# A two-layer graph network on one core: moving the addition of the edges' x from POOL's DMAs to VectorE

## The chip, the cores and the metric

The kernel runs on one core of one Trainium2 chip. The metric is the device time of one execution, in microseconds. Inputs and outputs lie in the chip's memory; intermediate tables are kept there too.

## What is computed

There are 100,000 nodes with rows of 64 fp32 numbers, and 25,000 edges (src, dst), sorted by dst. Two layers follow each other.

```
h = relu(layernorm(x))
# layer 0: attention over the incoming edges of a node, residual branch, batch norm over the nodes
score = sum(h[src] * h[dst]);  a = softmax of score over the edges of one dst
agg   = segment_sum((h @ W_conv + b_conv)[src] * a, dst)
r     = relu(h @ W_res + b_res)
x2    = x + batchnorm(agg + r) * gamma + beta
h2 = relu(layernorm(x2))
# layer 1: messages along the edges, summed at dst, combined with the node
m     = gelu(gelu([h2[src], h2[dst], edge_attr] @ W_m1 + b_m1) @ W_m2 + b_m2)
boxes = segment_sum(m, dst)
out   = x2 + h2 + gelu(gelu([h2, boxes] @ W_c1 + b_c1) @ W_c2 + b_c2)
```

## The kernel before

Nodes are worked in 49 steps of 2048 (the last has 1696: 106 partitions of 16 rows). Edges are worked in G = 49 groups: a group is 128 partitions by 4 edges; the last has 106 partitions. Each engine has its own program, in an order written out by hand, two steps or two groups a round; semaphores tie them together. There are three stages.

Stage A (0 to about 865 us) goes over all nodes and all edges of layer 0. SyncE (SP) loads x; VectorE (DVE) centres it and scales it; TensorE (PE) transposes and multiplies by W_res; ScalarE (ACT) applies relu, and stores r. For each group, GpSimd (POOL) issues eight indirect DMAs (`gather_x`, L605): for each of 4 edge columns the rows x[dst] and x[src], 128 rows of 256 bytes each, into a ring of GS = 8 tiles (`x_ring`, two of its own, two in `gout`, four in `part`). SP stores each ring tile to the table `edge_x` (`stash_x`, L433), and the edges' r goes to the table `edge_r`. DVE must have centred a ring tile before POOL may gather into it again (`E_ctr`, waited for in `gather_x`). The groups are taken from the last to the first. The attention sums of a group, divided (L838 to L842), stay in SBUF (`agg`). From the 31st group on, POOL also scatters them to the table `agg_rows` (`put_agg`, four indirect DMAs a group, L609), one group after each third group of gathers, and then 18 groups (`PUTS_AHEAD`) without any step between. An index above N - 1 marks a row that is left out, so the scatters, and in the kernel before also the gathers, carry a bounds check against a register.

Stage B (about 865 to 1375 us) goes over the nodes: x2, its layer norm, the two products of the combining network, and the output rows of all nodes as if they had no incoming edge. POOL adds h2 to x2 of the even steps (`add_h2`, L648) and between two such steps issues the rest of the scatters to `agg_rows`, and once all have landed, from 1107 us on, gathers agg[src] for the edges (`gather_agg`, four indirect DMAs a group) into a ring of 4; SP stores these to `edge_agg` (`stash_agg`, L538). POOL may gather into a ring slot when its store has landed.

Stage C (about 1375 us to the end) goes over the groups again. SP loads `edge_r` to `rr` (L510) and `edge_agg` to `agg_in` (L516). DVE's `scale_r` (L997, L999) adds agg[src] to the src half of `rr` and multiplies all of it by the batch norm's scale. Then POOL's `add_x` (L642) issues a direct DMA that adds the stored x rows to `rr` in SBUF; PE's `sum_edges` (L1553, L1556) waits for its landing (`C_x`), and sums `rr` and the filled agg of dst to x2 of the edges. DVE centres it (L772, L774), and the messages follow: PE products, ACT gelus, a scan on DVE along the sorted edges (L1033), and the combining network. POOL writes the finished rows of the dst nodes over `out` (`put_final`, L609, four scatters a group; `edge_final`, L1041, on DVE makes them ready). In POOL's loop over g the order is add_x(g), then gather_agg for a group 34 ahead, then up to two put_final per g from g = 15 on. The messages are summed with indices of `prev_row`, a table of flags loaded by SP (`load_prev`).

## Time and profile before

| | us |
|---|---|
| three runs | 1833.20, 1814.08, 1828.24 |
| their median | 1828.24 |
| the profiled execution | 1824.53 |
| its span, first to last instruction | 1822.7 |

The profiled execution's own time is 1.8 us above its span. In a profile PE is TensorE's matmuls, PEld its weight loads, DVE VectorE, ACT ScalarE, POOL GpSimd, SP SyncE; an engine's name with q is its sequencer, which issues DMAs. A row of a timeline gives start, duration, engine, line, operation, tiles, and in brackets how long the engine had been idle and what released it. "issue" means that the profile shows nothing that was waited for; "remote" or "another core or an unknown queue" that a semaphore was waited for whose update the profile can't put down to an instruction. POOL's busy time covers the making of a DMA's descriptors, not its transfer; there are 0.3 us between two indirect DMAs on POOL that count as idle.

### The profile page before, as it was taken

Reading aid. Unit: us, or ns where it says so; the run is one execution under the profiler, and the core shown is the slowest. Engines: PE = TensorE matmul, PEld = TensorE weight load, DVE = VectorE, ACT = ScalarE, POOL = GpSimd, SP = SyncE. Lnnn points to the kernel's source line nnn. Section 1 sums busy time; section 2 is a strip of 40 time slices with the busy share of each in tenths; the row PEclk is TensorE's granted clock in tenths of the full one; section 3 lists DMA queues with packets and bytes.
Section 4 is the critical chain, followed back from the end, with each engine's and each line's share of the span. In section 5 each row is a group of like instructions: output and inputs, shape, how many; then the busy total and the mean of one; then the engine's idle time right before and its main releaser. Section 6 shows DMA issues by size and latency. Waiting matters only on the chain.

```text
span 1822.7 us, 22166 instructions
## 1 busy us (share of the span) xinstructions
PE 1313.4 (72%) x6521; PEld 875.2 (48%) x6521; DVE 1351.0 (74%) x2253; ACT 927.7 (51%) x1840; POOL 1233.3 (68%) x1062
## 2 busy tenths in 40 slices
PE   3441756765737475275898898888885998899994
PEld 1231545554526354164666666566664443444431
DVE  7832776798649387187979998688854998799972
ACT  4511533453325242163666776476651776577772
POOL 7774664677765747500868887667867878887675
PEclk8755776786778676587888997798875999899996
DMA  7751764654435332125344554555555764566620
GB/s 216 258 177 34 285 231 155 209 200 141 117 95 166 100 114 90 36 99 220 110 160 157 194 185 161 163 176 189 174 160 127 183 162 121 133 146 156 139 49 16
DMA packets 132615, 273.56 MB, mean 150 GB/s; under 512 B 30404, under 2 KB 47658, under 8 KB 132496
## 3 DMA queue, kind: packets, MB, share of 16 engines
q1 hardware_dynamic: 76004, 187.38, 30.8%
q0 software_dynamic: 39360, 43.42, 12.0%
q10 hardware_dynamic: 17132, 41.35, 6.1%
q8 instruction: 54, 0.88, 0.2%
q14 instruction: 65, 0.53, 0.1%
HBM read 151.68 MB, written 121.80 MB: 150 GB/s over the span
## 4 chain that ended last, share of the span: by engine, by line
PE 29%; issue 24%; POOL 18%; another core or an unknown queue 10%; DVE 10%; ACT 5%; DMA 3%; ACTq 0%; SPq 0%; POOLq 0%; DVEq 0%
POOL agg_rows L609 11%; PE banks L1503 4%; POOL out L609 4%; PE banks L1387 3%; PE banks L1579 2%; DVE stat L772 2%; PE banks L1372 2%; PE banks L1577 2%; PE banks L1493 2%; PE banks L1586 2%; DVE stat L764 2%; PE banks L1553 2%; PE banks L1593 2%; POOL agg_ring L605 2%
## 5 line engine op out<-in xcount | busy, mean ns | idle before, releaser
L605 POOL DMA_INDIRECT part<-in_x,edge_idx x192 | 212.1, 1104 | 124.1 <-DVE part L774 66.3
L605 POOL DMA_INDIRECT agg_ring<-agg_rows,edge_idx x196 | 233.5, 1191 | 84.8 <-issue 56.4
L609 POOL DMA_INDIRECT agg_rows<-agg,put_first x196 | 232.2, 1185 | 58.0 <-issue 57.6
L609 POOL DMA_INDIRECT out<-agg,put_last x196 | 215.5, 1100 | 67.3 <-issue 59.8
L1503 PEld LDWEIGHTS banks<-packed,cT 97*128 97x128 f32 (+1 forms) x1568 | 216.3, 223 | 45.1 <-issue 45.1
L1372 PE MATMUL banks<-ident,xc 128*128 128x128 f32 (+1 forms) x784 | 137.6, 326 | 136.6 <-issue 76.4
L1503 PE MATMUL banks<-packed,cT 97*128 97x64 f32 (+1 forms) x1568 | 224.4, 309 | 0.0
L1099 ACT ACTIVATE hT<-banks 128x512 f32<-128x512 f32 (+1 forms) x98 | 55.5, 594 | 324.0 <-remote 165.4
L1387 PE MATMUL banks<-hT,packed 128*128 128x512 f32 (+1 forms) x196 | 132.2, 810 | 78.9 <-issue 54.3
L1372 PEld LDWEIGHTS banks<-ident,xc 128*128 128x128 f32 (+1 forms) x784 | 113.9, 177 | 147.5 <-issue 100.6
L1493 PE MATMUL banks<-hT,packed 64*96 64x512 f32 (+1 forms) x392 | 127.7, 730 | 59.6 <-ACT cT L1216 45.9
L605 POOL DMA_INDIRECT x_ring<-in_x,edge_idx x104 | 118.2, 1137 | 56.5 <-issue 34.1
L605 POOL DMA_INDIRECT gout<-in_x,edge_idx x96 | 106.0, 1104 | 45.1 <-issue 28.6
L764 DVE TENSOR_REDUCE stat<-sq 128x16 f32<-128x1024 f32 (+1 forms) x98 | 117.4, 1213 | 24.0 <-ACT sq L1091 19.4
L648 POOL TENSOR_TENSOR xt<-xt,xc 128x1024 f32<-128x1024 f32 (+1 forms) x19 | 49.2, 2589 | 120.9 <-DVE xc L778 120.6
L838 DVE RECIPROCAL inv<-banks 128x4 f32<-128x4 f32 (+1 forms) x49 | 8.7, 177 | 152.8 <-remote 134.4
L778 DVE SCALAR_TENSOR_TENSOR xc<-xc,stat 128x1024 f32<-128x1024 f32 (+1 forms) x98 | 117.1, 1217 | 1.7
L1091 ACT ACTIVATE sq<-xc 128x1024 f32<-128x1024 f32 (+1 forms) x98 | 102.8, 1049 | 29.9 <-issue 19.6
L772 DVE TENSOR_REDUCE stat<-xt 128x16 f32<-128x1024 f32 (+1 forms) x86 | 104.1, 1210 | 11.0 <-POOL xt L648 7.9
L774 DVE SCALAR_TENSOR_TENSOR xc<-stat,xt 128x1024 f32<-128x1024 f32 (+1 forms) x86 | 109.1, 1268 | 2.9
L1432 PE MATMUL banks<-agg,ones 128*128 128x256 f32 (+1 forms) x98 | 41.3, 512 | 91.1 <-DVE agg L842 88.0
L1215 ACT ACTIVATE cT<-banks,packed 96x512 f32<-96x512 f32 (+1 forms) x98 | 66.7, 681 | 76.6 <-PE banks L1493 72.7
(166 smaller groups left out, 3195.2 us busy)
## 6 DMA issues: line engine op xcount, KB each, us to landing
xt<-in_x SPq DMA_DIRECT2D x84, 512.0 KB
r_rows<-rT ACTq DMA_DIRECT2D x48, 512.0 KB
agg_rows<-rb SPq DMA_DIRECT2D x48, 512.0 KB
out<-xt SPq DMA_DIRECT2D x36, 512.0 KB
edge_r<-rr ACTq DMA_DIRECT2D x48, 256.0 KB
rT<-r_rows SPq DMA_DIRECT2D x24, 512.0 KB
part<-r_rows SPq DMA_DIRECT2D x24, 512.0 KB
rr<-edge_r SPq DMA_DIRECT2D x48, 256.0 KB
```

Source lines behind the costliest of these rows:

```text
L605: A.indirect_dma_start(to, None, table[:, :], bass.IndirectOffsetOnAxis(ap=idx, axis=0), bounds_check=limit, oob_is_err=False).then_inc(si ...
L609: A.indirect_dma_start(table[:, :], bass.IndirectOffsetOnAxis(ap=idx, axis=0), rows_of, None, bounds_check=limit, oob_is_err=False).then_i ...
L764: V.tensor_reduce(total, rows(squares), AX, ALU.add).then_inc(st.sem, 1)
L772: V.tensor_reduce(total, rows(source), AX, ALU.add).then_inc(st.sem, 1)
L774: V.scalar_tensor_tensor(out=rows(tile), in0=per_row(total), scalar=-1.0 / D, in1=rows(source), op0=ALU.mult, op1=ALU.add).then_inc(st.sem, 1)
L778: V.scalar_tensor_tensor(out=tile, in0=source, scalar=0.0, in1=per_row(deviation), op0=ALU.max, op1=ALU.mult).then_inc(st.sem, 1)
L1091: A.activation(sq[s % 2][0:p, :], xc[s % CS][0:p, :], ACT.Square).then_inc(st.sem, 1)
L1215: A.activation(blocks(cT[b][0:H2, 0, :], p), blocks(bank(4)[0:H2, :], p), ACT.Gelu, bias=bc1[:, :])
L1372: ins = T.transpose(to[:, c:c + p], xc[s % CS][0:p, c:c + P], ident[0:p, 0:p])
L1387: T.matmul(blocks(W[0][:, c], p), wres2[:, :], blocks(hT[:, c], p), start=True, stop=True)\
L1493: ins = T.matmul(blocks(bank(4 + i)[0:H2, :], p), wc1_node[i * D:i * D + D, :], blocks(hT[i * D:i * D + D, b * HALF:(b + 1) * HALF], p), s ...
L1503: ins = T.matmul(to[0:p, i * D:i * D + D], cT[b][:, i % 2, (i // 2) * P:(i // 2) * P + p], wc2[:, :], start=(i == 0), stop=(i == 7))
```

## The change

Three things are changed. In stage C, SP loads the stored x rows of a group to the first four tiles of the ring (`x_in`; the last two of them are in use by stage B until its last step), and DVE adds them to the scaled `rr` in a third instruction of `scale_r`; PE waits for DVE's count instead of the DMA, and POOL's 49 adding DMAs are gone. The gathers lose their bounds check, the scatters keep it. All indirect DMAs of the last group take 128 partitions instead of 106; the index table holds 0 for edges that don't exist, which the scatters leave out, and DVE sets the group's `agg` to zero at the start.

```diff
--- before.py
+++ after.py
@@ -203,6 +203,7 @@
         outT = [rT[1][:, q * EG:(q + 1) * EG] for q in range(2)]
         pairT = [sq[q // 2][:, (q % 2) * EG:(q % 2 + 1) * EG] for q in range(4)]
         x_ring = [sb(f"x_ring{q}", [P, EC]) for q in range(2)] + [gout[0][:, 0:EC], gout[0][:, EC:2 * EC]] + xe
+        x_in = x_ring[0:4]
         agg_in = [sb(f"agg_in{q}", [P, EW]) for q in range(MI)]
         agg_ring = [sb(f"agg_ring{q}", [P, EW]) for q in range(RS)]
 
@@ -294,12 +295,12 @@
 
         C_ld = Slots(E_st.sems, before=G)
         C_ga = slots("gathered_agg_loaded", MI)
-        C_x = slots("edge_x_added", 4)
+        C_x = slots("edge_x_loaded", 4)
         C_ea = slots("edge_attr_loaded", 4)
         C_sm = slots("same_prev_loaded", MS)
         C_ft = stage("agg_transposed")
         C_fs = stage("agg_filled")
-        C_ra = stage("edge_r_scaled", 2)
+        C_ra = stage("edge_r_scaled", 3)
         C_as = stage("edge_x2_summed")
         C_xd = stage("dst_x2_copied")
         C_f = stage("edge_x2_centered", 2)
@@ -515,6 +516,13 @@
                 sp.wait_ge(Y_st.of(g), Y_st.after(g))
                 sp.dma_start(agg_in[g % MI][0:p, :], edge_agg[g][0:p, :]).then_inc(C_ga.of(g), 16)
 
+            def load_edge_x(g):
+                C_ra.done(sp, g - 4)
+                if g in (2, 3):
+                    sp.wait_ge(B_fin.sem, B_fin.after(S - 1))
+                p = edges_of(g)
+                sp.dma_start(x_in[g % 4][0:p, :], edge_x[g][0:p, :]).then_inc(C_x.of(g), 16)
+
             def load_attr(g):
                 c = edges_of(g) * EJ
                 q = (g % 4) * DE
@@ -555,6 +563,8 @@
                     for g in range(2):
                         load_prev(g)
                     for g in range(6):
+                        if g < 2:
+                            load_edge_x(g)
                         if g < 4:
                             load_attr(g)
                             load_agg(g)
@@ -573,9 +583,11 @@
                 a = 2 * i
                 if i == 0:
                     for g in range(2, 4):
+                        load_edge_x(g)
+                    for g in range(2, 4):
                         load_prev(g)
-                for g, do in ((a + 4, load_agg), (a + 6, load_edges), (a + 5, load_agg), (a + 7, load_edges),
-                              (a + 4, load_prev), (a + 5, load_prev)):
+                for g, do in ((a + 4, load_agg), (a + 4, load_edge_x), (a + 6, load_edges), (a + 5, load_agg),
+                              (a + 5, load_edge_x), (a + 7, load_edges), (a + 4, load_prev), (a + 5, load_prev)):
                     if is_group(g):
                         do(g)
                 due = max(stashed, min(G, agg_groups(S - 1) - G + a + 3))
@@ -602,8 +614,7 @@
                 pool.reg_add(limit, nodes, -1)
 
             def gather(to, table, idx, signal):
-                A.indirect_dma_start(to, None, table[:, :], bass.IndirectOffsetOnAxis(ap=idx, axis=0),
-                                     bounds_check=limit, oob_is_err=False).then_inc(signal, 16)
+                A.indirect_dma_start(to, None, table[:, :], bass.IndirectOffsetOnAxis(ap=idx, axis=0)).then_inc(signal, 16)
 
             def scatter(table, idx, rows_of, signal):
                 A.indirect_dma_start(table[:, :], bass.IndirectOffsetOnAxis(ap=idx, axis=0), rows_of, None,
@@ -611,35 +622,27 @@
 
             def gather_x(n):
                 g = group_of(n)
-                p = edges_of(g)
                 E_ctr.done(pool, n - GS)
                 X_st.done(pool, n - GS)
                 waits_end()
                 for j in range(EJ):
                     for k, idx in enumerate((dst_idx, src_idx)):
                         c = (2 * j + k) * D
-                        gather(x_ring[n % GS][0:p, c:c + D], x, idx_of(idx, g, j, p), G_x.of(n))
+                        gather(x_ring[n % GS][:, c:c + D], x, idx_of(idx, g, j, P), G_x.of(n))
 
             def put_agg(n):
                 g = group_of(n)
-                p = edges_of(g)
                 G_p.done(pool, n - 4)
                 pool.wait_ge(E_f.sem, E_f.after(n))
                 waits_end()
                 for j in range(EJ):
-                    scatter(agg_rows, idx_of(put_first, g, j, p), agg_of(g, p)[:, j * D:(j + 1) * D], G_p.of(n))
+                    scatter(agg_rows, idx_of(put_first, g, j, P), agg_of(g, P)[:, j * D:(j + 1) * D], G_p.of(n))
 
             def gather_agg(g):
-                p = edges_of(g)
                 Y_st.done(pool, g - RS)
                 waits_end()
                 for j in range(EJ):
-                    gather(agg_ring[g % RS][0:p, j * D:(j + 1) * D], agg_rows, idx_of(src_idx, g, j, p), G_a.of(g))
-
-            def add_x(g):
-                p = edges_of(g)
-                C_ra.done(pool, g)
-                A.dma_start(rr[g % 6][0:p, :], edge_x[g][0:p, :], accum_op=ALU.add).then_inc(C_x.of(g), 16)
+                    gather(agg_ring[g % RS][:, j * D:(j + 1) * D], agg_rows, idx_of(src_idx, g, j, P), G_a.of(g))
 
             def add_h2(s):
                 p = nodes_of(s)
@@ -648,12 +651,11 @@
                 A.tensor_tensor(here, here, xc[s % CS][0:p, :], ALU.add).then_inc(B_y.sem, 1)
 
             def put_final(g):
-                p = edges_of(g)
                 C_put.done(pool, g - 4)
                 pool.wait_ge(C_fin.sem, C_fin.after(g))
                 waits_end()
                 for j in range(EJ):
-                    scatter(out, idx_of(put_last, g, j, p), agg_of(g, p)[:, j * D:(j + 1) * D], C_put.of(g))
+                    scatter(out, idx_of(put_last, g, j, P), agg_of(g, P)[:, j * D:(j + 1) * D], C_put.of(g))
 
             for n in range(G):
                 if n == 0:
@@ -680,7 +682,6 @@
             last = G - ahead
             put = 0
             for g in range(G):
-                add_x(g)
                 if is_group(g + ahead):
                     gather_agg(g + ahead)
                 if g == last:
@@ -718,6 +719,7 @@
                     st.part(dve, step, k[0])
                 return done
 
+            V.memset(agg_of(G - 1, P), 0.0)
             V.memset(bias16[:, :, :], 0.0)
             for b in range(2):
                 V.memset(cT[b][H2:H2 + 1, :, :], 1.0)
@@ -997,6 +999,9 @@
                 V.tensor_tensor(to, to, rows(agg_in[g % MI][0:p, :]), ALU.add).then_inc(C_ra.sem, 1)
                 dve.wait_ge(C_ra.sem, C_ra.after(g, 1))
                 V.tensor_tensor(here, here, cols(bn[0:p, 0, :], ER), ALU.mult).then_inc(C_ra.sem, 1)
+                dve.wait_ge(C_x.of(g), C_x.after(g))
+                dve.wait_ge(C_ra.sem, C_ra.after(g, 2))
+                V.tensor_tensor(rr[g % 6][0:p, :], rr[g % 6][0:p, :], x_in[g % 4][0:p, :], ALU.add).then_inc(C_ra.sem, 1)
 
             def fill_scan(g):
                 c_ = edges_of(g) * EJ
@@ -1549,7 +1554,7 @@
                 if g == 0:
                     pe.wait_ge(B_ht.sem, B_ht.after(S - 1))
                     pe.wait_ge(s_fill, 6)
-                pe.wait_ge(C_x.of(g), C_x.after(g))
+                pe.wait_ge(C_ra.sem, C_ra.after(g))
                 T.matmul(to, ident[0:p, 0:p], rr[g % 6][0:p, :], start=True, stop=False)
                 pe.wait_ge(C_fs.sem, C_fs.after(g))
                 for j in range(EJ):
```

## Rows read from the trace of the kernel before

**Rows 1.** The page's head: busy time of each engine, POOL by fortieths of the span.
```profile
PE 1313.4 (72%) x6521; PEld 875.2 (48%) x6521; DVE 1351.0 (74%) x2253; ACT 927.7 (51%) x1840; POOL 1233.3 (68%) x1062
...
POOL 7774664677765747500868887667867878887675
```
**Rows 2.** Windows: stages A and C, two stretches of A; PE, PEld, DVE, ACT, POOL busy, clock.
```profile
0.00:865.00 865.00, 478.46 (x2329) 370.07 (x2329) 580.65 (x1054) 327.72 (x644) 516.24 (x472) 0.71 0.46 155
...
1375.00:1823.00 448.00, 387.07 (x1468) 172.27 (x1468) 349.44 (x667) 276.71 (x711) 332.48 (x306) 0.91 0.53 125
...
680.00:764.00 84.00, 30.52 (x138) 23.93 (x136) 37.35 (x72) 13.54 (x27) 65.12 (x63) 0.58 0.23 75
764.00:860.00 96.00, 64.39 (x370) 53.38 (x370) 72.49 (x149) 45.56 (x89) 0.40 (x1) 0.80 0.39 146
```
**Rows 3.** Timeline of stage A: one DVE stall and POOL beside it, one ACT stall.
```profile
121.06 1.81 PE L1404 MATMUL banks<-packed,sums 65*128 65x65 f32 x8
169.23 0.18 DVE L838 RECIPROCAL inv<-banks 128x4 f32<-128x4 f32 x1 [49.12 <-remote]
164.26 1.00 POOL L605 DMA_INDIRECT part<-in_x,edge_idx  x1 [0.30 <-issue]
187.98 1.00 POOL L605 DMA_INDIRECT part<-in_x,edge_idx  x1 [22.72 <-DVE part L774]
751.79 0.60 ACT L1099 ACTIVATE hT<-banks 128x512 f32<-128x512 f32 x1 [43.09 <-remote]
763.43 0.97 POOL L609 DMA_INDIRECT agg_rows<-agg,put_first  x1 [0.30 <-issue]
```
**Rows 4.** Waits of DVE in stage A: total us, times, longest.
```profile
DVE inv L838 <- remote: 134.4, 9, 49.1
```
**Rows 5.** POOL's DMAs by tile: ns min/median/max, first and last start us.
```profile
L605 POOL DMA_INDIRECT part<-in_x,edge_idx x192: 991/997/2936, 57.5 to 682.7; - x192
L609 POOL DMA_INDIRECT agg_rows<-agg,put_first x196: 966/972/2826, 451.4 to 1100.0; - x196
L642 POOL DMA_DIRECT2D rr<-edge_x x49: 883/1003/1037, 1376.6 to 1747.0; - x49
```
**Rows 6.** POOL's timeline: of the last group (106 partitions): first and eighth gather, first and last scatter.
```profile
4.85 1.79 POOL L605 DMA_INDIRECT x_ring<-in_x,edge_idx  x1 [3.30 <-issue]
...
20.63 1.62 POOL L605 DMA_INDIRECT x_ring<-in_x,edge_idx  x1 [0.30 <-issue]
...
451.39 2.83 POOL L609 DMA_INDIRECT agg_rows<-agg,put_first  x1 [0.30 <-issue]
1815.62 1.56 POOL L609 DMA_INDIRECT out<-agg,put_last  x1 [0.31 <-issue]
```
**Rows 7.** PE's timeline at the opening of stage C: its waits for the adding DMA.
```profile
1386.96 2.04 PE L1553 MATMUL banks<-rr,ident 128*128 128x512 f32 x2 [12.76 <-DMA rr<-edge_x]
1402.10 1.19 PE L1553 MATMUL banks<-rr,ident 128*128 128x512 f32 x1 [7.37 <-DMA rr<-edge_x]
```
**Rows 8.** Windows of stage C: the stretch with stalls, and the steady one.
```profile
1500.00:1575.00 75.00, 63.57 (x234) 29.06 (x233) 56.19 (x107) 44.29 (x113) 60.12 (x57) 0.91 0.49 119
1600.00:1745.00 145.00, 144.57 (x583) 64.57 (x582) 136.01 (x255) 107.11 (x281) 109.87 (x102) 1.00 0.62 142
```
**Rows 9.** DVE's timeline in stage C: scale_r of three groups, idle gaps, the tail.
```profile
1494.71 0.69 DVE L999 TENSOR_TENSOR rr<-rr,bn 128x512 f32<-128x512 f32 x1
1615.99 0.69 DVE L999 TENSOR_TENSOR rr<-rr,bn 128x512 f32<-128x512 f32 x1
1642.55 0.69 DVE L764 TENSOR_REDUCE stat<-esq 128x8 f32<-128x512 f32 x1 [0.23 <-issue]
1737.22 0.69 DVE L999 TENSOR_TENSOR rr<-rr,bn 128x512 f32<-128x512 f32 x1
1779.45 0.69 DVE L764 TENSOR_REDUCE stat<-esq 106x8 f32<-106x512 f32 x1 [6.61 <-issue]
```
**Rows 10.** DVE adds in stage B, by tile: ns min/median/max, first and last start.
```profile
L961 DVE TENSOR_TENSOR xt<-xt,gout x37: 1210/1217/3940, 878.7 to 1374.0; 128x1024 f32<-128x1024 f32 x36, 106x1024 f32<-106x1024 f32 x1
```

## The prediction

> **What bounds the kernel now.** I read the page first. No engine is busy over 74% of the span, and the digits of POOL hang at 6 to 8 through all of it [rows 1]. That looks like slack and isn't: two indirect DMAs on POOL start 1.30 us apart, of which 1.00 counts as busy and 0.30 as idle [rows 3], so POOL issuing without a pause shows 77%.
>
> The windows by stage come next [rows 2]. Stage A is the worst: 865 us for 581 us of DVE and 478 of PE, the clock at 0.71 on average. The timeline shows why. PE's last matmul of L1404 ended by the profile at 122.9 us, yet DVE, which waits for it at L838, starts at 169.23, with 49 us put down to nobody. POOL had issued gathers without a gap until 164.26 + 1.00, and then waited for a ring slot [rows 3]. Late in the stage ACT stood for 43 us with POOL in a row of 72 scatters; these ended at 764.4, and then, with POOL idle (0.4 us busy of 96), DVE was busy 72 of 96 us, against 37 of 84 just before [rows 2, 3]. DVE's waits of this kind at L838 alone are 134 us in 9 times [rows 4]. So I read stage A as set by POOL's streams of indirect DMAs: while one runs, PE's semaphore updates arrive late, and each stall ends when POOL pauses. Why that is so the trace doesn't say.
>
> In stage C the steady stretch is different: PE busy 144.6 of 145 us, DVE 136.0 [rows 8]. L999 at 1615.99 and 1737.22 are 16 groups, 8 rounds, apart: 15.15 us a round [rows 9]. PE bounds it with DVE right behind. Before that, from 1500 to 1575, PE is busy only 63.6 of 75 us [rows 8].
>
> **Part 1: POOL's 49 adding DMAs go, SP loads, DVE adds.** Saved first:
> - The opening of stage C. PE waits 12.8 and then 7.4 us for the adding DMA [rows 7]. The x of groups 2 and 3 can't be loaded before stage B's last rows are ready, behind SP's stores of gathered agg, and DVE's in-order queue stands at its third add until they land: all four scale_r are ahead of the first fill_scan. So I leave the first wait as it is and take away the second, less 2 us of that queueing: -5 us.
> - The middle. Once the final scatters start, POOL issues 8 of them and one add per group, 8 x 1.27 + 1.3 = 11.5 us, for groups that come every 7.6 us. The eight groups after L999 at 1494.71 take to 1570.4, 75.7 us against 4 x 15.15 = 60.6: -15 us. With no add in its loop POOL can be late only for the output rows, which nobody on the chip waits for until the end.
> - The tail. POOL catches up its puts in one row after its last add at 1747 us [rows 5], and DVE stands for 6.6 us at L764 [rows 9]. With the adds gone the puts are not behind. I take half: -3 us.
>
> Added: 49 adds of 128x512 on DVE, both inputs in SBUF. The nearest row is L999, the same tile, 0.69 us [rows 9]; it depends on the one before, which costs a gap of 0.03 us: 0.72 each. Four stand ahead of the rounds where DVE waits for loads anyway; 45 in them. Two a round are 1.44 us. DVE's idle time in a round is (145 - 136.0) / 145 x 15.15 = 0.94 us, of which nine dependent steps of the inversion take some 0.3 at 0.03 each; 0.23 is a wait for ACT's square [rows 9] that an add standing ahead of it covers. I take 0.3 us of cover in all, so DVE becomes the bound at 15.15 + 1.14 = 16.3 us a round: 22.5 x 1.14 = +26 us. Ends: all idle time but the gaps covers (22.5 x 0.8 = +18), or none (45 x 0.72 = +32).
>
> SP's new loads stand behind nothing long: x of group a+4 waits for DVE's third instruction of group a, done two rounds earlier, and is issued before SP stops at load_edges. Behind it wait load_edges and load_prev of later groups, a round or more ahead of use. Bytes moved by DMA stay the same. I price this at 0; one late load of a few us a round is the upper end, and nothing below 0.
>
> The SBUF page of the Trainium skill (SBUF — State Buffer, on which operations grab the shared port pair) says that a DVE instruction with two SBUF inputs contends with a GpSimd one that reads SBUF, and the later blocks fully. L961, which has two, takes 1.22 us as a rule and up to 3.94 us in stage B, where POOL has adds of its own [rows 10]; that agrees. By that rule each new add could meet a POOL add and take 2.7 us more, but stage C has none, only DMAs, so the sum stays.
>
> Sum of part 1: -5 - 15 - 3 + 26 = +3 us.
>
> **Part 2: gathers without the bounds check.** 392 gathers in stage A, 196 later. The trace has no unchecked indirect DMA. The scatter, also checked, takes a median of 0.972 us against 0.997; the direct DMA, 128 rows of descriptors with no check and no index, has a median of 1.003 and a minimum of 0.883 [rows 5]. So the check is at most 0.11 us by the latter, 0.41 if the 0.30 us between indirect DMAs is its price too (the direct DMA starts without that gap), and less than nothing if the unchecked form is slower, by 0.03 at most as far as the forms differ here. I take 0.03 us, since the two kinds differ by no more. In stage A, which POOL sets: 384 x 0.03 = -11.5 us. In B the 136 gathers after 1107 us share the path with PE: half of 4, -2. In C they are hidden.
>
> **Part 3: a full last group.** With 106 partitions the eight first gathers took 1.79 to 1.62 us (15.3 in all), the first scatter 2.83 (7.7 with the three after it), the last of the kernel 1.56, as did the three before it to 0.03 [rows 6]. With 128 they should take 0.97 to 1.00. The gathers come to 8.0, so 7.3 less, of which I count half, since nodes alone fill the first three rounds: -3.5. First scatters: 7.7 - 3.9 = -4, in a POOL stream of stage A. Last four: 4 x 0.6 = -2.4, fully on the end. The memset at the start of DVE lies before the first x has landed: 0. Sum -10.
>
> **Sum.** 1824.5 + 3 - 13.5 - 10 = 1804, against the profiled execution's own time; that execution is 0.2% under the median of the three runs, 1828.2. I predict 1805 us. About 1% is what a measurement of this kernel can tell from no change (the runs before span 19 us).
>
> **Rivals.**
> 1. The check was dear. If the 0.30 us gap goes with it, stage A loses 384 x 0.30 = 115 us more than 0, B about 10: 1824.5 + 3 - 10 - 125 = 1690. At 0.1 us it is 38 + 5 + 10 - 3: 1770. For it: the gap stands ahead of indirect DMAs only. Against: scatter, gather and direct DMA take nearly the same time, and the gap may be the reading of the indices.
> 2. Slower: stage C gets stage A's disease. Today its indirect DMAs come in rows of 4 or 8 with a direct one between, and PE loses nothing in the steady stretch. Without it POOL issues rows as long as it has ready groups; about three groups are behind when the puts begin. In stage A, DVE lost 134 us at L838 over 764 us of POOL streams, 18%. Over the 274 us of final scatters (196 x 1.4) that would be +48, over half of them +24. With DVE's adds uncovered (+32), and nothing from the check: 1824.5 + 32 - 5 - 15 - 2.4 + 24 = 1858. It decides from the point where POOL is more than a group behind all through the stage. Against: production of a group takes 8 us and its puts 5.6, so POOL must pause in each round once it has caught up.
> 3. Break-even: stage A doesn't follow POOL after all (its stalls have another cause), the unchecked gather costs the same, and only part 1 and the tail count: 1824.5 + 3 - 2.4 = 1825.
>
> **Chances.** My forecast's own case 0.36 (1788 to 1818), rival 1 0.24, rival 2 0.22, rival 3 0.18. Faster by over 1% (below 1810) takes rival 1 and six tenths of my case: 0.46. Slower by over 1%: 0.22. Within: 0.32. The range runs from 1735, between rival 1's two figures, to 1856.
>
> **What would show it.** Stage C: L999's spacing 16.3 us a round instead of 15.15, DVE at 98% and PE near 92% in the steady stretch, no PE wait at L1553 over 5 us after the first. POOL: no L642; the last four scatters at 0.97 us; a median of L605 at 0.97 (0.7 or less, or a shorter gap, is rival 1). Stage A: POOL's last scatter of the row at 764 us moved to about 745, and DVE's waits for "remote" hardly changed. Waits of that kind in stage C for more than 10 us in all would be rival 2. I am wrong at the root if POOL's streams get shorter and stage A doesn't, or if the stalls go away with POOL as busy as before.

## The result and the profile after

| | kernel before | changed kernel |
|---|---|---|
| runs beside each other | 1814.08 to 1838.15 (4 runs) | 1957.00 to 1994.97 (4 runs) |
| median, us | 1830.72 | 1986.76 |
| the profiled execution, its span | 1824.53, 1822.7 | 1985.14, 1983.3 |

The ratio is 1.078, 95% interval 1.060 to 1.096: 8% slower, where I had predicted 1805 us. The same kernel before took 1603 to 1608 us in four of the five later comparisons and 1821 us in the fifth, so the kernels are met in two conditions, and, as the experiments show, the loss belongs to one of them. I call them the quick and the late condition. Both kernels above ran in the late one.

Rows of the page of the changed kernel, which answer to [rows 1]:

```profile
span 1983.3 us, 22167 instructions
PE 1361.3 (69%) x6521; PEld 898.0 (45%) x6521; DVE 1382.4 (70%) x2303; ACT 930.3 (47%) x1840; POOL 1107.6 (56%) x1013
POOL 7735555436564456501758666568566364554555
issue 24%; PE 23%; DVE 20%; another core or an unknown queue 16%; POOL 8%; ACT 7%; DMA 1%; DVEq 0%; ACTq 0%; SPq 0%; POOLq 0%
```

POOL has less to do (1107.6 us busy, 1233 before) and stands more. In the chain that ended last, 16% are waits that the profile can put down to nobody (10% before).

Windows by stage and one in the steady part of stage C (for [rows 2] and [rows 8]):

```profile
core 0: us, PE busy (x) PEld busy (x) DVE busy (x) ACT busy (x) POOL busy (x), PEclk, DMA share, GB/s
0.00:936.00 936.00, 495.27 (x2332) 375.52 (x2333) 584.65 (x1058) 327.62 (x644) 471.37 (x473) 0.71 0.42 143
936.00:1479.00 543.00, 469.14 (x2709) 346.84 (x2708) 416.85 (x530) 324.56 (x484) 376.49 (x289) 0.80 0.46 155
1479.00:1983.00 504.00, 396.85 (x1484) 175.64 (x1483) 380.92 (x716) 278.14 (x712) 259.75 (x253) 0.89 0.37 110
1700.00:1800.00 100.00, 93.23 (x369) 40.50 (x368) 94.96 (x181) 69.56 (x178) 52.50 (x51) 1.00 0.45 135
```

Stage A ends at about 936 us instead of 865. The windows here are cut near the stage's ends by eye; to compare kernels I take as the start of stage C in all of them the first start of DVE's multiplication in `scale_r` (L999 before, L1001 now). It is at 1375.6 us before and at 1483.3 now, so 108 us are lost ahead of stage C, and C itself, to the end of the span, takes 500 us instead of 447: +53. The two make the 160.6 us between the spans. No stage has more work to speak of: DVE's 1382.4 us are 31 more than before, and those are the new adds.

Waits of stage C that end by "remote", in the changed kernel (wait, us in total, times, longest):

```profile
ACT part L1315 <- remote: 32.8, 4, 11.4
DVE sums L1013 <- remote: 21.8, 5, 8.4
ACT sq L1280 <- remote: 17.9, 1, 17.9
DVE stat L774 <- remote: 13.0, 1, 13.0
DVE agg L1046 <- remote: 3.7, 1, 3.7
```

Together 89 us, counted for ACT and DVE apart though they partly overlap; the same view of the kernel before has 9.4 us (5.1, 3.5 and 0.8) between 1380 and 1823. The timeline shows the longest of them as the picture of [rows 3] over again, now in stage C:

```profile
1622.90 0.97 POOL L620 DMA_INDIRECT out<-agg,put_last  x1 [0.30 <-issue]
1624.18 0.97 POOL L620 DMA_INDIRECT out<-agg,put_last  x1 [0.30 <-issue]
1628.39 0.69 DVE L774 TENSOR_REDUCE stat<-banks 128x8 f32<-128x512 f32 x1 [12.97 <-remote]
1628.51 0.60 ACT L1280 ACTIVATE sq<-banks 128x512 f32<-128x512 f32 x1 [17.91 <-remote]
1629.16 2.00 PE L1584 MATMUL banks<-sq,packed 128*80 128x512 f32 x2 [16.13 <-ACT sq L1280]
```

POOL issues indirect DMAs without a pause from 1588.9 to 1625.15, 8 gathers and then 20 scatters; three engines stand for 13 to 18 us at its end (PE for ACT's result) and go on 3 us after POOL has stopped.

In stage A POOL itself shows the loss best. Up to its last scatter of the stage, at 829 us instead of 764, its waits for DVE to centre a ring tile, kernel before first, are:

```profile
POOL part L605 <- DVE part L774: 66.3, 5, 22.7
POOL x_ring L605 <- DVE part L774: 22.1, 1, 22.1
POOL gout L605 <- DVE part L774: 16.4, 2, 10.1
```

```profile
POOL gout L617 <- DVE part L776: 92.6, 5, 26.3
POOL part L617 <- DVE part L776: 79.7, 8, 24.0
POOL x_ring L617 <- DVE part L776: 47.7, 5, 25.4
```

That is 105 us before and 220 now: POOL is busy 45 us less in that stretch (471 against 516) and waits 115 us more.

### The profile page after: what moved, and what is told of

Its sections match the earlier page's. It is cut to its first block, busy times and chain, and to the rows that moved or that the text cites. A ratio compares the mean times of both kernels' runs of the same rounds, so it can differ in the third digit from the quotient of the medians.

```text
span 1983.3 us, 22167 instructions
## 1 busy us (share of the span) xinstructions
PE 1361.3 (69%) x6521; PEld 898.0 (45%) x6521; DVE 1382.4 (70%) x2303; ACT 930.3 (47%) x1840; POOL 1107.6 (56%) x1013
## 4 chain that ended last, share of the span: by engine, by line
issue 24%; PE 23%; DVE 20%; another core or an unknown queue 16%; POOL 8%; ACT 7%; DMA 1%; DVEq 0%; ACTq 0%; SPq 0%; POOLq 0%
PE banks L1508 7%; POOL agg_rows L620 6%; PE banks L1498 4%; DVE stat L766 3%; PE banks L1392 3%; PE banks L1377 3%; DVE stat L774 3%; DVE sums L1013 2%; DVE sq L1038 2%; DVE rr L1001 1%; ACT sq L1096 1%; ACT rT L1113 1%; ACT cT L1221 1%; POOL out L620 1%
## 5 line engine op out<-in xcount | busy, mean ns | idle before, releaser
L620 POOL DMA_INDIRECT out<-agg,put_last x196 | 204.1, 1041 | 172.5 <-DVE agg L1046 116.6
L617 POOL DMA_INDIRECT agg_ring<-agg_rows,edge_idx x196 | 216.2, 1103 | 119.5 <-DMA edge_agg<-agg_ring 62.2
L617 POOL DMA_INDIRECT part<-in_x,edge_idx x192 | 190.9, 994 | 135.8 <-DVE part L776 79.7
L620 POOL DMA_INDIRECT agg_rows<-agg,put_first x196 | 218.4, 1114 | 58.0 <-issue 57.7
L1508 PEld LDWEIGHTS banks<-packed,cT 97*128 97x128 f32 (+1 forms) x1568 | 226.0, 232 | 48.4 <-issue 48.1
L1508 PE MATMUL banks<-packed,cT 97*128 97x64 f32 (+1 forms) x1568 | 234.7, 318 | 0.5 <-issue 0.5
L1392 PE MATMUL banks<-hT,packed 128*128 128x512 f32 (+1 forms) x196 | 144.0, 866 | 125.0 <-ACT hT L1104 62.8
L617 POOL DMA_INDIRECT x_ring<-in_x,edge_idx x104 | 105.4, 1014 | 79.5 <-DVE part L776 47.7
L1392 PEld LDWEIGHTS banks<-hT,packed 128*128 128x128 f32 x196 | 47.3, 273 | 175.4 <-issue 98.4
L1113 ACT ACTIVATE rT<-banks,packed 128x512 f32<-128x512 f32 (+1 forms) x98 | 67.2, 686 | 95.2 <-remote 44.8
```

The costliest lines, as they stand in the source:

```text
L617: A.indirect_dma_start(to, None, table[:, :], bass.IndirectOffsetOnAxis(ap=idx, axis=0)).then_inc(signal, 16)
L620: A.indirect_dma_start(table[:, :], bass.IndirectOffsetOnAxis(ap=idx, axis=0), rows_of, None, bounds_check=limit, oob_is_err=False).then_i ...
L1113: A.activation(blocks(rT[s % 2][:, c], p), blocks(W[0][:, c], p), ACT.Relu, bias=bres2[:, :], accum_out=rsum[:, 2 * s + b:2 * s + b + 1]). ...
L1392: T.matmul(blocks(W[0][:, c], p), wres2[:, :], blocks(hT[:, c], p), start=True, stop=True)\
L1508: ins = T.matmul(to[0:p, i * D:i * D + D], cT[b][:, i % 2, (i // 2) * P:(i // 2) * P + p], wc2[:, :], start=(i == 0), stop=(i == 7))
```

## Experiments

There are eighteen runs, in five sets of three or four. The kernels of one set run on one chip beside the kernel before; chips are told apart by a number. The expectations use three theories: that stage A is set by POOL's rate of issue; that unbroken rows of indirect DMAs hold up the others' semaphore updates; and that the stalls belong to the place or condition of the run and not to the kernel.

### Set 1: the three parts alone (chip 8, kernel before 1607.48 us)

Part 2 alone, `e1_unchecked`:

```diff
 def gather(to, table, idx, signal):
-    A.indirect_dma_start(..., bass.IndirectOffsetOnAxis(ap=idx, axis=0), bounds_check=limit, oob_is_err=False)
+    A.indirect_dma_start(..., bass.IndirectOffsetOnAxis(ap=idx, axis=0))
```

> The kernel before with one edit: the gathers lose their bounds check. The profile of the changed kernel shows unchecked gathers at 0.947 us (0.997 checked), and stage A 69 us longer. Theory A (rate): gathers that follow each other faster, 1.25 us apart instead of 1.30, hold up TensorE's semaphore updates more; then stage A is 50 to 90 us longer here too, B some 20 to 35, and the time is 1890 to 1950. Theory B (rows): only long rows of indirect DMAs without anything else between them hold up the updates, and their length in stage A is the same; then stage A stays within 20 us of before or gets shorter by the gathers' 0.05 x 392 = 20 us, and the time is 1800 to 1840.

Measured: 1583.86 us, ratio 0.986 (0.983 to 0.989).

Part 1 alone, `e2_dve_add`: the kernel before with the hunks of the change that touch `x_in`, `C_x`, `C_ra`, `load_edge_x`, `add_x`, `scale_r` and PE's wait.

```diff
+    V.tensor_tensor(rr[g % 6][0:p, :], rr[g % 6][0:p, :], x_in[g % 4][0:p, :], ALU.add)
...
-    add_x(g)
```

> The kernel before with part 1 alone: SyncE loads x of the edges, VectorE adds it, no adding DMAs; gathers checked, last group as before. Theory B (rows): stages A and B as before; stage C about 50 us longer, of which 22.5 x 1.05 = 24 by VectorE's bound of 16.2 us a round and the rest by stalls where scatters stand in rows without a direct DMA: 1860 to 1890. Theory A (rate): no stalls in stage C, since nothing is faster: only the 24 us less the 20 us that the adding DMAs cost: 1820 to 1845.

Measured: 1618.5 us, ratio 1.007 (1.004 to 1.009).

The whole change but with checked gathers, `e3_after_checked` (the diff of `e1_unchecked` taken back in the changed kernel):

> The changed kernel with the bounds check put back on the gathers. Theory A (rate): stages A and B return to their times of before, and what is left is stage C: 1840 to 1890, about 100 us or more under the changed kernel. Theory B (rows): the check doesn't matter, 1960 to 2010.

Measured: 1611.06 us, ratio 1.002 (1.000 to 1.004).

Part 3 alone, `e4_full_group`:

```diff
-    p = edges_of(g)
+    p = P
...
+    V.memset(agg_of(G - 1, P), 0.0)
```

(in `gather_x`, `put_agg`, `gather_agg` and `put_final`).

> The kernel before with one edit: the indirect DMAs of the last group take 128 partitions. By the prediction 10 us shorter (first gathers, first and last scatters of 0.97 us instead of 1.6 to 2.8): 1810 to 1825. A rival: POOL starts its first row of gathers earlier and closer together while the first loads are under way, and stage A gets longer by its stalls, over 1850.

Measured: 1596.96 us, ratio 0.994 (0.993 to 0.996), 10.5 us less than before.

What follows: the kernel before itself is 223 us quicker than it was in the first measurement, and here the parts do about what their sizes say. An unchecked gather is 0.05 us shorter. The first row is of the tile `part` in `e4_full_group` (checked), the second in `e1_unchecked` (min/median/max in ns):

```profile
L605 POOL DMA_INDIRECT part<-in_x,edge_idx x192: 992/997/2937, 48.9 to 584.8; - x192
```

```profile
L605 POOL DMA_INDIRECT part<-in_x,edge_idx x192: 941/947/2367, 52.1 to 567.7; - x192
```

392 such gathers in stage A at 0.05 us are 20 us of the 23.6 measured. Part 1 beside part 3 costs 14 us here (`e3_after_checked` less `e4_full_group`).

### Set 2: the change as it is, the change without part 1, and short breaks (chip 11, kernel before 1606.88 us)

`a1_after` is the changed kernel. `b1_combo` is the kernel before with parts 2 and 3 only. `a2_after_breaks` puts a small operation ahead of every four indirect DMAs, 245 in all:

```diff
+    def short_break():
+        if breaks[0]:
+            pool.wait_ge(s_pause, breaks[0])
+        breaks[0] += 1
+        A.memset(pause[:, :], 0.0).then_inc(s_pause, 1)
```

> The changed kernel itself, beside the kernel before, on the chip of this call. On the chip of the first four runs the kernel before took 1607 us instead of 1830, and its stage A 633 us instead of 865, without the late semaphore updates. Theory C (the stalls belong to the chip and state it runs in, and the change makes them worse only where they are): on a chip without them the changed kernel is at 0.985 to 0.992 of before (0.986 for the check times 1.002 for the rest); on one with them at 1.05 to 1.10. Rival D (the three edits together do harm on any chip): over 1.02 in any case.

Measured: 1576.88 us, ratio 0.982 (0.980 to 0.983).

> The kernel before with the unchecked gathers and the full last group, but POOL's adding DMAs kept. Without stalls the two gains add up: 0.986 x 0.994 = 0.980 of before. With stalls, and if the rows of scatters that the missing adding DMAs leave are what hurts in stage C: stage C as before, and stage A whatever the unchecked gathers do there, 1.00 to 1.05.

Measured: 1577.24 us, ratio 0.981 (0.979 to 0.982).

> The changed kernel with a memset of an unused tile of 8 columns, waiting for the one before, ahead of every four indirect DMAs on POOL. Theory B (rows): where there are stalls they are shorter or gone, 5% or more under the changed kernel in the same call. Rival: the breaks only cost POOL about 245 x 0.3 = 70 us, most of it hidden without stalls: 0 to 2% over the changed kernel.

Measured: 1582.81 us, ratio 0.985 (0.982 to 0.987).

So the very kernel that was 8% slower is 1.8% faster than the kernel before here. Its windows by stage and in the steady part of C:

```profile
core 0: us, PE busy (x) PEld busy (x) DVE busy (x) ACT busy (x) POOL busy (x), PEclk, DMA share, GB/s
0.00:641.00 641.00, 442.22 (x2355) 348.69 (x2355) 588.28 (x1063) 331.72 (x651) 497.33 (x473) 0.82 0.62 209
641.00:1123.00 482.00, 424.99 (x2701) 316.63 (x2701) 414.52 (x531) 316.21 (x479) 382.00 (x283) 0.87 0.53 175
1123.00:1572.00 449.00, 378.30 (x1468) 165.47 (x1466) 375.42 (x711) 278.64 (x711) 266.47 (x259) 0.94 0.42 123
1400.00:1500.00 100.00, 93.30 (x370) 40.86 (x370) 95.02 (x180) 69.76 (x177) 52.51 (x50) 1.00 0.42 121
```

Stage A takes 641 us with POOL busy 497.33; 464 indirect DMAs, each with 0.30 us ahead of it, make that 636 of 641. POOL issues them in one unbroken row, and DVE is busy 588 of the 641 us beside it. Among the waits of this execution not one ends by "remote". The steady window is that of the late condition, to 0.2 us.

The breaks of `a2_after_breaks` turn out to be none. `c3_before_breaks` of set 3, which has the same memsets in the kernel before, shows one:

```profile
201.80 1.00 POOL L607 DMA_INDIRECT x_ring<-in_x,edge_idx  x1 [0.30 <-issue]
202.79 0.13 POOL L620 MEMSET pause<- 128x8 f32 x1
203.11 1.71 POOL L607 DMA_INDIRECT x_ring<-in_x,edge_idx  x1 [0.19 <-issue]
```

The memset lies inside the 0.30 us that stand ahead of every indirect DMA. The median from the end of one indirect DMA to the start of the next is 0.305 us with a memset between them and 0.305 us without, in `a2_after_breaks`, `c3_before_breaks` and `f3_after_breaks` alike. So POOL's rows went on unbroken in these three.

### Set 3: parts and breaks again (chip 5, kernel before 1608.27 us)

`c3_before_breaks` has the same short breaks in the kernel before. The others are repeats.

> The kernel before with part 1 alone: x rows loaded by SyncE, added by VectorE. Two answers, by whether this chip shows the late semaphore updates. If the kernel before takes about 1830 us here (late updates present): the theory that POOL's rows of indirect DMAs with no adding DMA or wait between them hold up PE's updates says this part alone carries most of the loss, ratio 1.05 to 1.09 (it takes away the x_ring waits, 105 down to 18, that broke POOL's rows). The rival, that the rows of gathers merely come faster when unchecked, says 1.00 to 1.02 here and the loss in the second kernel. If the kernel before takes about 1607 us: 1.007 again, as in the first comparison.

Measured: 1621.09 us, ratio 1.009 (1.006 to 1.012).

> The kernel before with unchecked gathers and the full last group, adding DMAs kept. If the kernel before takes about 1830 us: the theory of pure rows says 0.98 to 1.00 (the breaks by x_ring waits stay), the rival of faster gathers says 1.05 to 1.09. If it takes about 1607 us: 0.981 again.

Measured: 1572.54 us, ratio 0.978 (0.975 to 0.981).

> The kernel before with one small POOL memset of an unused tile (waiting for the memset before it) ahead of every pair to four indirect DMAs. If the kernel before takes about 1830 us: the theory that unbroken rows on POOL hold up the semaphore updates says stage A falls by a large part of the 220 us between the chips, 1650 to 1750 us; the rival, that it is the indirect DMAs' number and not their order, says 1830 to 1850. If the kernel before takes about 1607 us: the breaks cost the same 6 us as in the changed kernel, 1610 to 1616.

Measured: 1610.97 us, ratio 1.002 (1.000 to 1.004).

> The changed kernel with the same breaks. If the kernel before takes about 1830 us: the theory of unbroken rows says that the 1987 us of the changed kernel fall to below 1850; the rival says 1970 to 2000. If it takes about 1607 us: 1583 again, ratio 0.985.

Measured: 1584.34 us, ratio 0.986 (0.983 to 0.989). It is the quick condition again, which leaves the question of the late one as it was.

### Set 4: does POOL set stage A? (chip 2, kernel before 1603.59 us)

`d3_long_breaks` makes six chained memsets of each break:

```diff
+                for _ in range(6):
+                    if breaks[0]:
+                        pool.wait_ge(s_pause, breaks[0])
+                    breaks[0] += 1
+                    A.memset(pause[:, :], 0.0).then_inc(s_pause, 1)
```

> The kernel before with six chained POOL memsets of an unused tile, some 1.2 us or more, ahead of every four indirect DMAs. If the kernel before takes about 1830 us: if pauses of POOL let the late updates through, stage A gets shorter in spite of the added work, 1700 to 1780; if not, 1900 or more. If it takes about 1607 us, this measures how far POOL's issuing sets stage A there: if it sets all of it (98 pauses before the gathers and some 30 before scatters in stage A, 1.2 to 1.8 us each), 150 to 230 us more, 1760 to 1840; if DVE sets it (284 of 300 us busy with unchecked gathers), under 100 more.

Measured: 1755.21 us, ratio 1.093 (1.087 to 1.098).

> The kernel before with part 1 alone, for a chip with the late semaphore updates. If the kernel before takes about 1830 us here: the theory of unbroken rows says 1.05 to 1.09, the rival of faster gathers 1.00 to 1.02. If it takes about 1607 us: 1.006 to 1.010 for the third time.

Measured: 1624.38 us, ratio 1.011 (1.008 to 1.015).

> The kernel before with unchecked gathers and the full last group, adding DMAs kept. If the kernel before takes about 1830 us: the theory of unbroken rows says 0.98 to 1.00, the rival of faster gathers 1.05 to 1.09. If it takes about 1607 us: 0.978 to 0.982.

Measured: 1571.18 us, ratio 0.979 (0.976 to 0.983).

> The changed kernel. If the kernel before takes about 1830 us: 1.06 to 1.10, as at first. If it takes about 1607 us: 0.980 to 0.984.

Measured: 1581.57 us, ratio 0.986 (0.983 to 0.990).

The windows of `d3_long_breaks` by stage, against those of `e4_full_group`, which has no breaks (670, 485 and 438 us):

```profile
0.00:762.00 762.00, 456.12 (x2405) 362.26 (x2405) 588.25 (x1062) 336.93 (x655) 605.75 (x1153) 0.78 0.53 176
762.00:1302.00 540.00, 456.08 (x2649) 340.97 (x2650) 422.77 (x534) 315.12 (x474) 438.94 (x703) 0.78 0.48 158
1302.00:1762.00 460.00, 388.91 (x1468) 174.09 (x1468) 342.71 (x657) 277.21 (x711) 369.10 (x677) 0.91 0.49 118
```

Stage A has some 680 memsets more (1153 against 474 instructions), POOL is busy 80 us more than the 525.5 of `e4_full_group`, and the stage is 92 us longer with DVE and PE doing the same work. In it POOL waits for another engine once, for 0.3 us. POOL does set stage A in the quick condition. The price that was expected of a break was too high: six chained memsets widen the gap between two indirect DMAs from 0.305 to 1.08 us, 0.8 us and not 1.2 to 1.8. So stage A alone gave 92 us where 150 to 230 were expected of it; stage B (55 us) and stage C (22 us) bring the whole near the low end.

### Set 5: the late condition (chip 11 again, kernel before 1820.58 us)

> The kernel before with part 1 alone. If the kernel before takes about 1830 us here: the theory of unbroken rows says 1.05 to 1.09, the rival of faster gathers 1.00 to 1.02. If it takes about 1607 us: 1.006 to 1.011 again.

Measured: 1903.23 us median, 1861.76 to 1916.64, 1.045 times the median of the kernel before (the quickest of the four runs 1.02 times). The four runs lie 55 us apart and give no interval; by the median the time is under the 1.05 of the one theory and over the 1.02 of the other.

> The kernel before with the two other parts. If the kernel before takes about 1830 us: the theory of unbroken rows says 0.98 to 1.00, the rival of faster gathers 1.05 to 1.09. If it takes about 1607 us: 0.978 to 0.981.

Measured: 1894.78 us, ratio 1.041 (1.032 to 1.051).

> The changed kernel with a small memset on POOL ahead of every four indirect DMAs. If the kernel before takes about 1830 us: the theory of unbroken rows says below 1850, the rival 1970 to 2000. If it takes about 1607 us: 0.985 again.

Measured: 1972.25 us, ratio 1.086 (1.076 to 1.096).

Chip 11 had been quick in set 2, so the condition is no fixed property of a chip; the results name the chip and not which of its cores ran. `b1_combo` and `f2_combo` are one and the same kernel on the same chip, 1577.24 and 1894.78 us. The first 110 us of both, `b1_combo` first:

```profile
0.00:110.00 110.00, 54.20 (x223) 35.67 (x224) 93.12 (x156) 58.33 (x111) 83.69 (x87) 0.81 0.74 250
```

```profile
0.00:110.00 110.00, 31.24 (x72) 14.12 (x72) 48.61 (x82) 28.48 (x52) 82.65 (x88) 0.66 0.51 160
```

POOL does the same in both, one row of indirect DMAs. Beside it PE gets 223 matmuls done in the one and 72 in the other, DVE 156 instructions and 82. The granted clock is lower in the second, 0.66 against 0.81, but PE is busy in only 31 of the 110 us there, so the clock is not what it lacks. The timeline of `f2_combo` shows how:

```profile
107.03 0.94 POOL L605 DMA_INDIRECT x_ring<-in_x,edge_idx  x1 [0.30 <-issue]
108.28 0.94 POOL L605 DMA_INDIRECT x_ring<-in_x,edge_idx  x1 [0.30 <-issue]
108.45 0.69 ACT L1108 ACTIVATE rT<-banks,packed 128x512 f32<-128x512 f32 x1 [5.44 <-remote]
109.13 1.04 ACT L1091 ACTIVATE sq<-xc 128x1024 f32<-128x1024 f32 x1
110.08 0.62 ACT L1129 ACTIVATE esq<-part 106x512 f32<-106x512 f32 x1
110.21 1.22 DVE L764 TENSOR_REDUCE stat<-sq 128x16 f32<-128x1024 f32 x1 [39.23 <-ACT sq L1091]
```

From 76 to 108 us ACT gets one activation done in 5 to 10 us, with idle gaps of 4.1 to 9.9 us; the activations themselves take their usual 0.6 to 0.7 us. POOL ends at 109.22 because DVE, which waits for ACT, has not centred its next ring tile, and from then on ACT goes on without a gap for 5 us. POOL's next gather starts at 126.73. I read it as a loop: POOL's row holds up the others until it lacks their results itself.

The DMA view differs too. For most DMAs of `b1_combo` it has the median time from issue to landing; the line of the same DMAs in `f2_combo` has none. Its trace holds 11573 records of landings and that of `b1_combo` 27178; the five late traces have 10926 to 12053, the fifteen quick ones 27151 to 27244.

```profile
r_rows<-rT ACTq DMA_DIRECT2D x48, 512.0 KB, 2.9
agg_ring<-agg_rows,edge_idx POOLq DMA_INDIRECT x196, 3.5
```

```profile
r_rows<-rT ACTq DMA_DIRECT2D x48, 512.0 KB
agg_ring<-agg_rows,edge_idx POOLq DMA_INDIRECT x196
```

So "remote" in a late trace says that the record of an update is not there, and not by itself that the update came late; that the engines stood idle is in the records of their instructions. The transfers were not slower: the packets of the two large DMA queues took 34.8% and 13.8% of 16 engines' span of 1577.1 us in `b1_combo`, and 29.4% and 11.5% of 1888.7 us in `f2_combo`, which is 766 and 772 us. A rival by which other traffic slows the memory in the late condition has therefore little room.

The three kernels of the set by stage. Stage C of `f2_combo`, then of `f1_dve_add`, then of `f3_after_breaks`:

```profile
1458.00:1888.00 430.00, 386.94 (x1468) 170.83 (x1466) 343.72 (x657) 276.77 (x711) 321.25 (x299) 0.93 0.53 125
```

```profile
1413.00:1907.00 494.00, 404.38 (x1468) 177.29 (x1468) 377.99 (x712) 277.86 (x711) 268.89 (x252) 0.88 0.39 112
```

```profile
1458.00:1963.00 505.00, 407.42 (x1468) 175.53 (x1468) 379.74 (x716) 277.48 (x711) 264.85 (x315) 0.87 0.37 109
```

For the table stage C starts at DVE's first multiplication in `scale_r`, as above. The last column is POOL's longest row of indirect DMAs in the part of stage C up to the last multiplication.

| late condition | start of C, us | stage C, us | "remote" waits in C, us | longest row |
|---|---|---|---|---|
| kernel before | 1376 | 447 | 9 | 8 |
| parts 2 and 3 (`f2_combo`) | 1446 | 443 | 8 | 8 |
| part 1 (`f1_dve_add`) | 1411 | 496 | 73 | 40 |
| all and memsets (`f3_after_breaks`) | 1459 | 505 | 76 | 32 |
| all (changed kernel) | 1483 | 500 | 89 | 28 |

In stage C the loss belongs to part 1: the two kernels with the adding DMAs take 443 and 447 us, the three without them 496 to 505. In these POOL's rows of indirect DMAs are longer, and the "remote" waits come with them. Ahead of stage C the loss belongs to parts 2 and 3 together: 1376 and 1411 us without them, 1446 to 1483 with them. (Up to there the program of `f1_dve_add` is the kernel before's, so the 36 us between the first two are no effect of part 1, but the spread between executions.) Each row is one execution, and that of `f1_dve_add`, with 1908.91 us, is one of its long ones; but the other two kernels with part 1 agree with it in stage C, and the ratio of `f2_combo` by its runs, 1.032 to 1.051, is clear of the spread. The expectation that unbroken rows alone carry the loss, with `f2_combo` at 0.98 to 1.00, fell; so did its rival, which would have let part 1 off.

`f3_after_breaks` was to be below 1850 us if breaks helped, and took 1972. But its memsets lie in the gaps that were there anyway and break no row, so it says nothing of what a true pause would do; the six chained memsets of `d3_long_breaks`, which do make one, were met only by the quick condition. What the adding DMAs gave was, it seems, a wait: POOL stood at each for DVE's scaled rr. That reading was not tested by itself.

## Why the prediction was wrong

**The root.** I wrote that I would be wrong "at the root if POOL's streams get shorter and stage A doesn't, or if the stalls go away with POOL as busy as before". Both came. The gathers' median went from 0.997 to 0.947 us and stage A grew by some 70 us; POOL's last scatter of the stage, forecast at about 745 us, came at 829. And in the quick condition POOL issued 464 indirect DMAs in a row, busier than ever, with no "remote" wait at all. The reading of [rows 3] holds for the late condition as a description: POOL's row and the others' stalls go together there. The step that failed is the one after it: "stage A, which POOL sets: 384 x 0.03". POOL did save its time, 45 us of busy time up to its last scatter of the stage, and then waited 220 us for DVE instead of 105. In the late condition it doesn't set the stage alone; the engines that it waits for stand still beside its rows, and a shorter DMA does not bring their work forward. Where POOL's rate does set the stage (set 4) the step holds: -23.6 us against -13.5, by the size of 0.05 us for 0.03.

**Part 1.** DVE's bound was right. Two L1001 of the changed kernel in the quick condition, six rounds apart, are 97.24 us, 16.21 a round (16.3 predicted):

```profile
1402.75 0.69 DVE L1001 TENSOR_TENSOR rr<-rr,bn 128x512 f32<-128x512 f32 x1
1499.99 0.69 DVE L1001 TENSOR_TENSOR rr<-rr,bn 106x512 f32<-106x512 f32 x1
```

DVE at 95% and PE at 93% of the steady window; I had said 98 and 92. The new adds (L1004) took a median of 0.69 us and at most 0.694, in both conditions, beside rows of indirect DMAs. The Trainium skill (SBUF — State Buffer, on the shared port pair) warns of contention with a GpSimd instruction that reads SBUF. It did not come up; POOL has no adds in this stage.

The sum, +3 us, measured +11, +13 and +21 us alone (sets 1, 3 and 4), +14 beside part 3 (set 1), and beside both other parts 0 and +10 (`a1_after` less `b1_combo`, `d4_after` less `d2_combo`). In the profiles of three pairs (`a1_after` and `b1_combo`, `d4_after` and `d2_combo`, `e3_after_checked` and `e4_full_group`) DVE's first and last multiplications lie 5, 4 and 12 us further apart with part 1, where the opening's -5, the middle's -15 and the bound's +26 made it +6. The opening gave nothing: the seventh group's multiplication comes 36.5 us after the first with part 1 and 34.1 to 35.5 without. The tail behind them is 74.0, 74.0 and 73.6 us without part 1 and 71.6, 74.7 and 74.8 with it, so the -3 of the tail did not come.

In the late condition the step "with no add in its loop POOL can be late only for the output rows" is what failed: with the adds in the loop POOL's rows ahead of the tail were at most 8 indirect DMAs long, without them 28 to 40, and stage C grew by 49 us (`f1_dve_add`) and 53 us (the changed kernel).

**Part 2.** The price was bounded from both sides and taken at 0.03 us; it is 0.05, and the 0.30 us gap stays. The sign is right in the quick condition. In the late one parts 2 and 3 together cost +74 us of the kernel's time; how much of it is part 2's no run shows.

**Part 3.** -10 predicted, -10.5 measured alone. The last scatters take 0.97 us as forecast:

```profile
1974.51 0.97 POOL L620 DMA_INDIRECT out<-agg,put_last  x1 [0.31 <-issue]
```

**Rivals.** Rival 2, "stage C gets stage A's disease", came true, with the sign by which I said it would show (over 10 us of such waits in C; there are 89). It was priced at +24 to +48 us of stalls from 18% of a row. Against the same kernel in the quick condition, DVE's last multiplication of the stage comes 46 us later after its first in the changed kernel (425.5 us against 379.3) and 39 us later in `f1_dve_add` (against `e2_dve_add`); the kernel before loses 3 us by the same measure (against `e4_full_group`). That its price fits is in part luck, as it spread the stalls over all 274 us of scatters. Its place was right, its reason against was half right: POOL does pause in each round once it has caught up, and from 1665 us on nothing more is lost; all of the 46 us lie in the first 180 us of the stage, and 27 of them beside the row of 28 indirect DMAs that ends at 1625. Rival 1 fell, the check is 0.05 us; by its own terms its two figures are 1692 and 1774 us, where I wrote 1690 and 1770, and the range ended at 1856, just under the 1858 of rival 2. What I had no rival for is that parts 2 and 3, the plain gains, would cost more than part 1. I had let rival 3 say only that stage A might not follow POOL; I should have asked in which direction it could go, since the profile said of the stalls that nobody was waited for.

**What stays open.** What brings a core into the late condition, and by what path POOL's indirect DMAs then hold up the others, no run shows; that they do is read from traces, as no late run took the row away or broke it. Every run on record comes with a span and a granted clock, so it was recorded while it ran, and more than half of the landing records are missing in the late ones; whether the recording has a part in the stalls is untested. The runs can't tell part 2 from part 3 in the late condition either, as only both together ran there, so it isn't shown that 0.05 us less a gather lengthens the stalls, or why it would.

**A version that beats both.** Parts 2 and 3 without part 1 took 1571.18 us on chip 2, where the changed kernel took 1581.57 and the kernel before 1603.59; on chip 11 it and the changed kernel were the same (1577.24 and 1576.88). In the late condition it is 1.04 times the kernel before and the changed kernel 1.08: no version that ran beats the kernel before there.

## What to carry to other kernels

When a profile shows engines that stand for semaphores which nobody is seen to give, beside an engine that issues DMAs in a row, look first how long that engine itself waits for the others (here 105 us in stage A, 0.3 us in the quick condition). While it does, a shorter instruction on it is no gain to be multiplied by its count. Measure the kernel before once more before explaining a change against it: here the same program took 1607 and 1821 us, and the change is 2% faster in the one case and 8% slower in the other. A slow step that makes an engine wait for its consumers (here an adding DMA behind a semaphore) may be what keeps its rows short, so look for what it held back before taking it away. And when a break is put into a row, check in the trace that the row got longer: the memsets here fitted into a gap that was there already.

## What the runs showed that I had not expected

- The same chip is met in two conditions at different times: 1577 and 1895 us for one program, 1607 and 1821 us for the kernel before. In the late one a row of indirect DMAs on POOL goes with PE, ACT and DVE getting a third to a half of their instructions done (72 matmuls against 223 in the first 110 us), and more than half of the landing records are missing from the trace (11573 against 27178).
- An indirect DMA without a bounds check takes 0.947 us of POOL, with one 0.997; the 0.30 us ahead of it stay.
- A chained memset of 128x8 ahead of every four indirect DMAs, 245 of them, costs 3 us of 1608 in the kernel before and about 6 in the changed one, though POOL sets stage A: it takes about 0.12 us and hides in the 0.30 us ahead of the next indirect DMA.
- 8 gathers and 56 final scatters in one row in stage C (1210 to 1297 us in `a1_after`) hold up nobody in the quick condition; a row of 8 gathers and 20 scatters cost 27 us in the late one.
